# Windowed attention, then a spiking layer: the row-maximum matmuls cut into 64 by 64 tiles and moved ahead of the values, loops written out, and another order of one engine's transfers

## The chip, the cores and the metric

The kernel runs on one core of one Trainium2 chip. The metric is the device time of one execution in microseconds (us). Three runs of the kernel before gave 540.75, 542.55 and 543.64 us; the median is 542.55.

## The reference

The input `x` is (8, 32, 32, 256). Two layers follow each other, each added to its input, each behind a group norm (32 groups of 8 channels, over a whole sample).

```
qkv = part @ qkv_w.T + qkv_b            # part: 8 x 8 windows, 128 windows of 64 tokens, 256 channels
attn = einsum('wihd,wjhd->whij', q * SCALE, k) + bias_table[REL_IDX] + MASK     # 16 heads of 16
out  = softmax(attn) @ v                # per window and head
x = x + out
h = einsum('tbld,hd->tblh', x_normed, W) + b    # t is the sample, 8 steps
# v = v + (h - v) / 2;  spike = v >= 1;  v = 0 where it spiked;  x = x + spike
```

The spikes are thresholds, so the first layer is computed with 16-bit values split into a high and a low part.

## The kernel before

**Tiling.** Channels lie on the 128 partitions in two halves (`HALVES`). A *row* is one row of windows: 4 windows of 64 tokens, 256 tokens; there are 4 rows in a sample and 32 in all. A row is worked on as two *pairs* of windows, so the main loop has 64 pairs, `n`; `k` counts the 8 pairs of a sample, `p` is `k % 2`. In `run`, sample 0 and samples 6 and 7 are written out and samples 1 to 5 are a loop of the engines (`eng.Fori`). Behind the pairs comes the spiking layer, in `lif_units`, looped in the same way by `over_y`.

**Engines.** Each engine has its own program in a fixed, hand-written order; semaphores tie them. In pair `n` TensorE (PE) runs: the projections of the next row (q and k where `p` is 0, v where it is 1), `scores(n)`, the values of the pair before (`weigh_values(n - 1)`, L1005), the maxima's scores of the next pair (`max_scores(n + 1)`, L949 and L955), and the turning of an attention result (L1015). The softmax needs each query's maximum before the exponential: `max_scores` computes scores from the high parts alone with queries on the partitions, VectorE (DVE) reduces them (`maxima`, L756), PE turns the result (L989, in the middle of `scores`), ScalarE (ACT) copies it to `max_rows` (L570), and 8 matmuls with `pick_max` (L982) subtract it from the scores. ACT then takes two exponentials for each of the two banks (L579, L580), and GpSimd (POOL) makes the low part (L426).

**Transfers.** `scores` multiplies stacks of 96 partitions: 32 rows each of the parts high, low, high of q against high, high, low of k. SyncE (SP) builds them: it writes q and k of the next row to memory (`q_spill`, `k_spill`), spreads q's high part into `q_hi` for `max_scores` (4 issues), and reads the stacks back (`q_stack`, `k_stack`, 3 issues each). `scores` of a row's first pair waits on `stacked`; `max_scores` of it on `q_spread`. All these go through one queue, and x of the sample after next (L332) follows on it.

**Norms.** Once in a sample the statistics of the next one run beside pairs k = 1 to 3; POOL takes the roots at k = 2 (`norm_roots`), ahead of `xn_lo` (L388), for which the q projection waits.

## Time and profile before

| | |
|---|---|
| median of 3 runs | 542.55 us |
| the profiled execution, its time | 539.22 us |
| the profiled execution, its span | 537.5 us |
| PE busy | 455.3 us, 85% of the span |
| DVE, ACT, POOL busy | 429.5, 394.3, 272.7 us |
| PE's granted clock, mean | 0.978 |

Times in the rows are microseconds from the start of the span unless they are marked ns. A row of a timeline has start, duration, engine, line, operation and tiles, and in brackets the idle time of that engine before it and what ended it. Matmul durations hold the time through the array; the pace of back-to-back matmuls is the distance of their starts. PEld is the weight load of PE. "SPq" rows are the issues of transfers by SyncE.

### The profile page before, as it was taken

To read this page: it belongs to the slowest core of one execution; us is meant where nothing else is said; L and a number is where in the kernel's file an instruction comes from. 1 tells how busy PE (TensorE), PEld (TensorE's weight loads), DVE (VectorE), ACT (ScalarE), POOL (GpSimd) and SP (SyncE) were. 2 spreads that over 40 slices of the span, in tenths; PEclk is the share of its full clock that TensorE was granted. 3 is DMA by queue.
4 is the path that set the end of the run, shared out by engine and by line. 5 is a ranking of instruction groups with operands and counts; after the bars stand their busy time and mean duration, and the time that the engine had idled before them with its cause. 6 is when DMAs were issued, how large, how long until landed. Compare 5 with 4: busy or idle time off the path is not lost.

```text
span 537.5 us, 17535 instructions
## 1 busy us (share of the span) xinstructions
PE 455.3 (85%) x6504; PEld 417.5 (78%) x6504; DVE 429.5 (80%) x864; ACT 394.3 (73%) x885; POOL 272.7 (51%) x370
## 2 busy tenths in 40 slices
PE   0274799888999899989998998999899977789996
PEld 0164688888889788978887887898788866678885
DVE  8856568877888788878887898789777877488887
ACT  1375568877888788878887888788888856665551
POOL 6132466557555756666656566665655555540000
PEclk9988779999999999999999999999999989999999
DMA  6257066676777667767776778675666655023333
GB/s 194 80 153 194 8 177 175 165 201 171 186 180 180 173 180 185 211 149 209 198 198 161 195 195 200 159 190 157 160 160 168 163 142 157 3 84 132 137 137 138
DMA packets 92574, 86.07 MB, mean 160 GB/s; under 512 B 41842, under 2 KB 63604, under 8 KB 92532
## 3 DMA queue, kind: packets, MB, share of 16 engines
q1 hardware_dynamic: 91808, 85.49, 59.5%
q8 instruction: 27, 0.44, 0.4%
q10 hardware_dynamic: 724, 0.01, 0.1%
q14 instruction: 15, 0.12, 0.1%
HBM read 47.72 MB, written 33.55 MB: 151 GB/s over the span
## 4 chain that ended last, share of the span: by engine, by line
PE 37%; issue 16%; POOL 15%; ACT 9%; DVE 9%; DMA 8%; SPq 4%; POOLq 1%; ACTq 0%; DVEq 0%
POOL p_lo L426 7%; PE pv_ps L1005 4%; DMA k_stack<-k_spill1lo 3%; POOL xn_lo L388 3%; PE score_ps L982 3%; POOL xc L415 3%; PE proj_ps L905 3%; DMA k_spill1lo<-k_lo 3%; PE proj_ps L892 3%; PE pv_ps L892 3%; PE score_ps L892 3%; PE proj_ps L907 3%; PE proj_ps L906 3%; SPq L311 2%; PE max_ps L955 2%
## 5 line engine op out<-in xcount | busy, mean ns | idle before, releaser
L426 POOL TENSOR_TENSOR p_lo<-probs,p_hi 128x512 f16<-128x512 f32 x128 | 146.6, 1166 | 150.8 <-ACT p_hi L580 150.8
L579 ACT ACTIVATE probs<-score_ps 128x512 f32<-128x512 f32 x128 | 77.0, 601 | 18.4 <-PE score_ps L982 17.6
L905 PE MATMUL proj_ps<-xn_hi,w_hi 128*128 128x256 f32 x256 | 77.3, 302 | 14.2 <-POOL xn_lo L388 14.2
L972 PE MATMUL score_ps<-both_parts,bias_k 128*128 128x64 f16 x1024 | 78.2, 193 | 10.7 <-DMA k_stack<-k_spill1lo 6.3
L972 PEld LDWEIGHTS score_ps<-both_parts,bias_k 128*128 128x128 f16 x1024 | 69.7, 98 | 15.8 <-issue 7.8
L756 DVE TENSOR_REDUCE neg_max<-max_ps 128x16 f16<-128x1024 f32 x64 | 78.4, 1224 | 4.2 <-PE max_ps L955 2.1
L974 PE MATMUL score_ps<-q_stack,k_stack 96*128 96x64 f16 x1024 | 77.9, 193 | 0.0
L580 ACT ACTIVATE p_hi<-score_ps 128x512 f16<-128x512 f32 x128 | 77.4, 605 | 0.0
L906 PE MATMUL proj_ps<-xn_lo,w_hi 128*128 128x256 f32 x256 | 74.1, 290 | 0.0
L907 PE MATMUL proj_ps<-xn_hi,w_lo 128*128 128x256 f32 x256 | 73.4, 287 | 0.0
L974 PEld LDWEIGHTS score_ps<-q_stack,k_stack 96*128 96x128 f16 x1024 | 69.1, 98 | 0.0
L739 DVE SCALAR_TENSOR_TENSOR k_lo<-proj_ps,parity_mask,k_hi 128x512 f16<-128x512 f32 x64 | 45.1, 747 | 27.6 <-ACT k_hi L494 27.6
L750 DVE TENSOR_TENSOR v_lo<-proj_ps,v_hi 64x256 f16<-64x256 f32 x128 | 53.9, 421 | 12.9 <-ACT v_hi L502 10.8
L905 PEld LDWEIGHTS proj_ps<-xn_hi,w_hi 128*128 128x128 f32 x256 | 50.5, 197 | 15.9 <-POOL xn_lo L388 9.0
L502 ACT ACTIVATE v_hi<-proj_ps 64x256 f16<-64x256 f32 x128 | 50.3, 393 | 9.2 <-PE proj_ps L917 7.7
L770 DVE TENSOR_TENSOR attn<-pv_ps,recip 64x256 f32<-64x256 f32 x128 | 54.0, 422 | 3.1
L1005 PE MATMUL pv_ps<-v_hi,p_hi 128*128 128x68 f16 x512 | 55.9, 197 | 0.5 <-POOL p_lo L426 0.5
L1005 PE MATMUL pv_ps<-v_hi,p_lo 128*128 128x68 f16 x512 | 56.1, 197 | 0.0
L1005 PE MATMUL pv_ps<-v_lo,p_hi 128*128 128x68 f16 x512 | 56.0, 196 | 0.0
L982 PE MATMUL score_ps<-max_rows,pick_max 128*128 128x128 f16 x512 | 40.6, 224 | 18.1 <-ACT max_rows L570 16.4
L494 ACT ACTIVATE k_hi<-proj_ps,parity_mask 128x512 f16<-128x512 f32 x64 | 40.5, 684 | 20.0 <-PE proj_ps L907 20.0
L949 PE MATMUL max_ps<-bias_q,ident_h 128*128 128x512 f16 x128 | 50.0, 391 | 3.7 <-ACT bias_q L510 3.7
(137 smaller groups left out, 1349.3 us busy)
## 6 DMA issues: line engine op xcount, KB each, us to landing
xc<-in_x_dram SPq DMA_DIRECT2D x32, 256.0 KB, 4.8
k_stack<-k_spill0hi SPq DMA_DIRECT2D x32, 256.0 KB, 4.2
k_stack<-k_spill1hi SPq DMA_DIRECT2D x32, 256.0 KB, 4.0
out_dram<-xc SPq DMA_DIRECT2D x32, 256.0 KB, 2.3
q_hi<-q_flat SPq DMA_DIRECT2D x128, 32.0 KB, 2.0
k_spill0hi<-k_hi SPq DMA_DIRECT2D x16, 256.0 KB, 2.2
k_spill0lo<-k_lo SPq DMA_DIRECT2D x16, 256.0 KB, 2.4
q_stack<-q_spill0hi SPq DMA_DIRECT2D x32, 128.0 KB, 2.7
```

The lines of the kernel that those rows point to most:

```text
L426: pool.tensor_tensor(p_lo[p][:, quads, :, :].rearrange("p g w i -> p (g w i)"), probs[:, quads, :, :].rearrange("p g w i -> p (g w i)"), p ...
L579: act.activation(probs[:, quads, :, :].rearrange("p g w i -> p (g w i)"), score_ps[:, h, :], ACT.Exp)
L580: act.activation(p_hi[p][:, quads, :, :].rearrange("p g w i -> p (g w i)"), score_ps[:, h, :], ACT.Exp)\
L756: dve.tensor_reduce(neg_max[:, 0:16], max_ps[:, :, :].rearrange("p w (n j) -> p (w n) j", j=WS), AX.X, ALU.max, negate=True).then_inc(neg_ ...
L770: last = dve.tensor_tensor(attn[k % 2][rows, :, :, :], heads[rows, :, w, :, 0:D], recip[rows, :, w, :].unsqueeze(3).to_broadcast([WS, HALV ...
L905: pe.matmul(dst, w_hi[:, c, cols], high[:, tok], start=(c == 0 and bias is None), stop=False)
L906: pe.matmul(dst, w_hi[:, c, cols], low[:, tok], start=False, stop=False)
L907: last = pe.matmul(dst, w_lo[:, c, cols], high[:, tok], start=False, stop=(c == HALVES - 1))
L972: pe.matmul(dst, bias_k[:, variant(k, w), h * QUADS + g, :], both_parts[:, 0, :], start=(g == 0 and w == 0), stop=False)
L974: pe.matmul(dst, k_stack[slot][:, g, at, :], q_stack[slot][:, g, at, :], start=False, stop=False)
L982: last = pe.matmul(dst, pick_max[:, 4 * w + 2 * h + mid, :], max_rows[p][:, :].rearrange("p (q i) -> p q i", q=2), start=False, stop=(w == ...
L1005: last = pe.matmul(cols[:, :, g, :], pp[p][:, h * QUADS + g, :, :].rearrange("p w i -> p (w i)"), vv[k // 2][:, p, h * QUADS + g, :, :, :] ...
```

## The change

Four things change together.

1. `max_scores` and the `pick_max` matmuls are cut into tiles of 64 by 64: the contraction runs over one half of the partitions and the output lies on one half. The two halves of the partitions (pairs of quads, `mid`) now write two different banks of `max_ps` and of `score_ps`, where before a bank held a window or a half of the heads. The 2 bias matmuls of 512 columns and 8 of 128 become 8 of 256 and 16 of 128; the 8 `pick_max` matmuls of 128 columns become 16. `bias_q`, `pick_max` and the reading patterns of DVE and ACT are laid out to match.
2. On PE `max_scores(n + 1)` runs right behind the `pick_max` matmuls, ahead of `weigh_values(n - 1)`; on DVE `maxima(n + 1)` runs ahead of `attention_out(n - 1)`. The waits of both tile groups stand before the last ordinary matmul of `scores`.
3. `run` and `over_y` are written out: no engine loops any more.
4. SP's order in `move_q_and_k`: k's high part is spilled between the spreads of two quads each, and the stacks are read in the order q high twice, k high twice, q low, k low, each with a semaphore of its own.

```diff
-            for k in range(BODY):
-                body(k, k // 2, k, 0)
-            with eng.Fori(1, SAMPLES - 2) as s:
-                for k in range(BODY):
-                    body(s * BODY + k, s * WROWS + k // 2, k, s)
-            for s in (SAMPLES - 2, SAMPLES - 1):
+            for s in range(SAMPLES):
                 for k in range(BODY):
                     body(s * BODY + k, s * WROWS + k // 2, k, s)
...
+                landed = slot_total(row, y, 16)
                 sp.wait_ge(q_flat_done, done)
...
+                sp.dma_start(q_spill[slot][0], q_flat[:, 0, :]).then_inc(q_hi_spilled[slot], 16)
+                spread((0, 1))
                 sp.wait_ge(q_lo_done, done)
...
+                sp.dma_start(q_spill[slot][1], q_flat[:, 1, :]).then_inc(q_lo_spilled[slot], 16)
+                sp.wait_ge(k_hi_done, done)
+                spill_k(0, k_hi, k_hi_spilled)
+                spread((2, 3))
+                sp.wait_ge(k_lo_done, done)
+                spill_k(1, k_lo, k_lo_spilled)
+                sp.wait_ge(q_hi_spilled[slot], landed)
+                stack(0, q_stack[slot], q_spill[slot][0])
+                stack(2, q_stack[slot], q_spill[slot][0])
+                sp.wait_ge(k_hi_spilled[slot], landed)
+                stack(0, k_stack[slot], k_spill[slot][0])
+                stack(1, k_stack[slot], k_spill[slot][0])
+                sp.wait_ge(q_lo_spilled[slot], landed)
+                stack(1, q_stack[slot], q_spill[slot][1])
+                sp.wait_ge(k_lo_spilled[slot], landed)
+                stack(2, k_stack[slot], k_spill[slot][1])
...
-                dve.tensor_reduce(neg_max[:, 0:16], max_ps[:, :, :].rearrange("p w (n j) -> p (w n) j", j=WS), AX.X, ALU.max,
+                dve.tensor_reduce(neg_max[:, :].rearrange("p (m n) -> p m n", m=2)[:, :, 0:8],
+                                  max_ps[:, :, :].rearrange("p m (n j) -> p m n j", j=WS), AX.X, ALU.max,
...
+            def max_scores(k):
+
+                slot = k // 2 % 2
+                halves = [slice(r * WS, (r + 1) * WS) for r in range(2)]
                 for w in range(2):
...
+                    for mid, rows in enumerate(halves):
+                        for q, queries in enumerate(halves):
+                            pe.matmul(max_ps[queries, mid, w * 256:(w + 1) * 256], ident_h[rows, rows],
+                                      bias_q[rows, variant(k, w), q, :, :].rearrange("p h n -> p (h n)"),
+                                      start=(w == 0), stop=False)
+                for w in range(2):
                     wx = 2 * (k % 2) + w
                     for h in range(HALVES):
...
+                        at = (2 * w + h) * 128
+                        for mid, rows in enumerate(halves):
+                            for q, queries in enumerate(halves):
+                                last = pe.matmul(max_ps[queries, mid, at:at + 128], q_hi[slot][rows, h, wx, 2 * mid + q, :],
+                                                 k_hi[slot][rows, h, wx, :, :].rearrange("p e j -> p (e j)"),
+                                                 start=False, stop=(w == 1 and h == 1))
...
+                                if (mid, h, q, w) == (1, 1, 1, 1):
+                                    before_tiles()
+                                pe.matmul(dst, k_stack[slot][:, 2 * mid + q, at, :], q_stack[slot][:, 2 * mid + q, at, :],
+                                          start=False, stop=False)
...
+                        for mid, rows in enumerate(halves):
+                            for e, keys in enumerate(halves):
+                                dst = score_ps[keys, mid, :].rearrange("p (h q w i) -> p h w q i", h=2, q=2, w=2)[:, h, w, :, :]
+                                last = pe.matmul(dst, pick_max[rows, 2 * w + h, keys],
+                                                 max_rows[p][rows, :].rearrange("p (q i) -> p q i", q=2),
+                                                 start=False, stop=(w == 1 and h == 1))
+                            if w == 1 and h == 1:
+                                last.then_inc(score_ps_done, 1)
```

**Order on PE, end of `scores` of a pair.** `score_ps`, `max_ps` and `pv_ps` are the banks of the scores, of the maxima's scores and of the values. Before:

```order
L974 MATMUL score_ps<-q_stack,k_stack 128x64
L982 MATMUL score_ps<-max_rows,pick_max 128x2x64 [waits max_rows_done]
L982 MATMUL score_ps<-max_rows,pick_max 128x2x64 x7
L1005 MATMUL pv_ps<-v_hi,p_hi 128x2x34 [waits attn_done,p_lo_done]
...
L949 MATMUL max_ps<-bias_q,ident_h 128x512 [waits bias_q_done,max_rows_done]
L955 MATMUL max_ps<-k_hi,q_hi 128x128 x4
```

and the same place now:

```order
L997 MATMUL score_ps<-q_stack,k_stack 128x64 [waits bias_q_done,max_rows_done]
L1007 MATMUL score_ps<-max_rows,pick_max 64x2x64 x16
L966 MATMUL max_ps<-bias_q,ident_h 64x256 x8
L975 MATMUL max_ps<-k_hi,q_hi 64x128 x16
L1031 MATMUL pv_ps<-v_hi,p_hi 128x2x34 [waits attn_done,p_lo_done]
```

The two tile groups stand together, the wait for `max_rows` has moved one matmul forward, and the values come behind both.

**Order on DVE, a pair with the norm's variances.** `neg_max` is the reduction of the maxima, `root_guess` the start of POOL's roots, `recip` and `attn` the division of the values. Before:

```order
L739 SCALAR_TENSOR_TENSOR k_lo<-proj_ps,parity_mask,k_hi 128x8x64
L689 TENSOR_SCALAR tiny<-pv_ps 128x2 [waits norm_pe,pv_ps_done]
L692 TENSOR_SCALAR root_guess<-tiny 128x2 [waits norm_dve]
L766 RECIPROCAL recip<-pv_ps 128x32
L770 TENSOR_TENSOR attn<-pv_ps,recip 64x256 [waits recip_done]
L770 TENSOR_TENSOR attn<-pv_ps,recip 64x256
L756 TENSOR_REDUCE neg_max<-max_ps 128x16 [waits max_ps_done]
```

and now:

```order
L750 SCALAR_TENSOR_TENSOR k_lo<-proj_ps,parity_mask,k_hi 128x8x64
L767 TENSOR_REDUCE neg_max<-max_ps 128x2x8 [waits max_ps_done]
L699 TENSOR_SCALAR tiny<-pv_ps 128x2 [waits norm_pe,pv_ps_done]
L702 TENSOR_SCALAR root_guess<-tiny 128x2 [waits norm_dve]
L778 RECIPROCAL recip<-pv_ps 128x32
```

The reduction has moved ahead of everything that needs the values' bank.

**Order on SP, the transfers of one row.** Before:

```order
L308 DMA q_spill0hi<-q_flat 128x512 [waits q_flat_done]
L311 DMA q_hi<-q_flat 32x8x64 x4
L314 DMA q_spill0lo<-q_flat 128x512 [waits q_lo_done]
L317 DMA k_spill0hi<-k_hi 128x1024 [waits k_hi_done]
L317 DMA k_spill0lo<-k_lo 128x1024 [waits k_lo_done]
L303 DMA q_stack<-q_spill0hi 32x4x512 [waits q_spilled0]
L303 DMA q_stack<-q_spill0lo 32x4x512
L303 DMA q_stack<-q_spill0hi 32x4x512
L303 DMA k_stack<-k_spill0hi 32x4x1024 [waits k_spilled0]
L303 DMA k_stack<-k_spill0hi 32x4x1024
L303 DMA k_stack<-k_spill0lo 32x4x1024
```

and now:

```order
L314 DMA q_spill0hi<-q_flat 128x512 [waits q_flat_done]
L304 DMA q_hi<-q_flat 32x8x64 x2
L317 DMA q_spill0lo<-q_flat 128x512 [waits q_lo_done]
L308 DMA k_spill0hi<-k_hi 128x1024 [waits k_hi_done]
L304 DMA q_hi<-q_flat 32x8x64 x2
L308 DMA k_spill0lo<-k_lo 128x1024 [waits k_lo_done]
L298 DMA q_stack<-q_spill0hi 32x4x512 [waits q_hi_spilled0]
L298 DMA q_stack<-q_spill0hi 32x4x512
L298 DMA k_stack<-k_spill0hi 32x4x1024 [waits k_hi_spilled0]
L298 DMA k_stack<-k_spill0hi 32x4x1024
L298 DMA q_stack<-q_spill0lo 32x4x512 [waits q_lo_spilled0]
L298 DMA k_stack<-k_spill0lo 32x4x1024 [waits k_lo_spilled0]
```

The number of issues is the same; k's high part leaves two issues earlier, half of the spread leaves later, and no read of a high part waits for the write of a low one.

## Rows read from the trace of the kernel before

**Rows 1.** The page: busy time, share of the span, instructions.

```profile
PE 455.3 (85%) x6504; PEld 417.5 (78%) x6504; DVE 429.5 (80%) x864; ACT 394.3 (73%) x885; POOL 272.7 (51%) x370
```

**Rows 2.** Waits of the whole execution: us in total, times, longest.

```profile
PEld score_ps L982 <- ACT max_rows L570: 23.0, 40, 5.1
...
PE proj_ps L905 <- POOL xn_lo L388: 14.2, 8, 6.8
...
PE max_ps L989 <- DVE neg_max L756: 7.5, 9, 1.8
...
PE score_ps L972 <- DMA k_stack<-k_spill1lo: 6.3, 7, 2.3
...
PE score_ps L972 <- DMA k_stack<-k_spill0lo: 4.0, 4, 2.2
```

**Rows 3.** Timeline of PE, one row of windows inside the loop.

```profile
249.71 0.20 PE L972 MATMUL score_ps<-both_parts,bias_k 128*128 128x64 f16 x1
...
250.75 0.19 PE L974 MATMUL score_ps<-q_stack,k_stack 96*128 96x64 f16 x1
251.36 0.62 PE L982 MATMUL score_ps<-max_rows,pick_max 128*128 128x128 f16 x8 [0.41 <-ACT max_rows L570]
251.82 0.20 PE L1005 MATMUL pv_ps<-v_hi,p_hi 128*128 128x68 f16 x1
...
252.57 0.38 PE L949 MATMUL max_ps<-bias_q,ident_h 128*128 128x512 f16 x1
...
253.45 0.39 PE L1015 MATMUL proj_ps<-ident,attn 128*128 128x128 f32 x2
...
256.43 0.62 PE L982 MATMUL score_ps<-max_rows,pick_max 128*128 128x128 f16 x8
```

**Rows 4.** Timeline of ACT, the same stretch.

```profile
249.90 1.27 ACT L494 ACTIVATE k_hi<-proj_ps,parity_mask 128x512 f16<-128x512 f32 x2 [0.55 <-PE proj_ps L907]
251.06 0.25 ACT L570 ACTIVATE max_rows<-max_ps 16x128 f16<-16x128 f16 x1
```

**Rows 5.** Timeline of DVE, a pair with the norm's variances.

```profile
228.83 1.22 DVE L756 TENSOR_REDUCE neg_max<-max_ps 128x16 f16<-128x1024 f32 x1
```

**Rows 6.** Timeline of POOL, around the roots of a sample.

```profile
226.47 2.28 POOL L426 TENSOR_TENSOR p_lo<-probs,p_hi 128x512 f16<-128x512 f32 x2 [3.90 <-ACT p_hi L580]
...
233.03 1.26 POOL L388 TENSOR_TENSOR xn_lo<-xn,xn_hi 128x512 fp32r<-128x512 f32 x1
```

**Rows 7.** Timeline of PE: the q projection behind the roots, three samples.

```profile
131.52 0.38 PE L905 MATMUL proj_ps<-xn_hi,w_hi 128*128 128x256 f32 x1 [1.18 <-POOL xn_lo L388]
...
183.39 0.38 PE L905 MATMUL proj_ps<-xn_hi,w_hi 128*128 128x256 f32 x1 [1.18 <-POOL xn_lo L388]
...
234.35 0.38 PE L905 MATMUL proj_ps<-xn_hi,w_hi 128*128 128x256 f32 x1 [1.18 <-POOL xn_lo L388]
```

**Rows 8.** Timeline of SP: one row's transfers, inside the loop.

```profile
249.38 0.34 SPq L308 DMA_DIRECT2D q_spill0hi<-q_flat  x1
249.77 2.57 SPq L311 DMA_DIRECT2D q_hi<-q_flat  x4
...
254.39 0.32 SPq L303 DMA_DIRECT2D q_stack<-q_spill0hi  x1
...
255.88 0.78 SPq L303 DMA_DIRECT2D k_stack<-k_spill0hi  x2
256.71 0.43 SPq L303 DMA_DIRECT2D k_stack<-k_spill0lo  x1
```

**Rows 9.** Timeline of SP: one row's transfers, code written out.

```profile
375.61 0.34 SPq L308 DMA_DIRECT2D q_spill0hi<-q_flat  x1
...
378.90 1.82 SPq L314 DMA_DIRECT2D q_spill0lo<-q_flat  x1
...
384.57 0.44 SPq L303 DMA_DIRECT2D k_stack<-k_spill0lo  x1
```

**Rows 10.** The page, DMA issues: xcount, KB each, us from issue to landing.

```profile
k_stack<-k_spill0lo SPq DMA_DIRECT2D x16, 256.0 KB, 5.1
```

More of the change, by code:

```diff
@@ L251, in over_y @@
         def over_y(eng, body):
-            body(0)
-            with eng.Fori(1, WROWS - 1) as y:
+            for y in range(WROWS):
                 body(y)
-            body(WROWS - 1)
         BODY = 2 * WROWS
@@ L304, in stack, with spread, spill_k @@
                                  src.rearrange("(g r) n -> r g n", g=QUADS)).then_inc(stacked[slot], 16)
+                def spread(quads):
+                    for g in quads:
+                        rows = slice(32 * g, 32 * g + 32)
+                        sp.dma_start(q_hi[slot][rows, :, :, g, :].rearrange("p h w i -> p (h w) i"),
+                                     q_flat[rows, 0, :].rearrange("p (n i) -> p n i", i=WS)).then_inc(q_spread[slot], 16)
+                def spill_k(part, keys, spilled):
+                    sp.dma_start(k_spill[slot][part], keys[slot][:, :, :, :, :].rearrange("p h w e j -> p (h w e j)"))\
+                      .then_inc(spilled[slot], 16)
@@ L634, in _ @@
             dve.wait_ge(mask_step, 6)
-            dve.tensor_copy(pick_max[:, :, :].rearrange("p v (e j) -> p (v e) j", e=2),
-                            ident_h[:, 0:16].unsqueeze(2).to_broadcast([128, 16, WS]))
+            for r in range(2):
+                half = slice(r * WS, (r + 1) * WS)
+                dve.tensor_copy(pick_max[half, :, :].rearrange("p v (e j) -> p (v e) j", e=2),
+                                ident_h[half, r * WS:r * WS + 8].unsqueeze(2).to_broadcast([WS, 8, WS]))
             for buf in (v_hi[1], v_lo[1]):
@@ L776, in _ @@
             bias_variant(1)
-            q_low(1)
+            q_low(0, 1)
             k_low(0, 1)
@@ L806, in pair @@
                     norm_moments(norm, x1_stats, SAMPLES - 1)
+                if not is_last_pair(n):
+                    maxima(n + 1)
                 beside = None
@@ L951, in max_scores @@
                     wx = 2 * (k % 2) + w
                     for h in range(HALVES):
-                        for mid in range(2):
-                            at = (2 * h + mid) * 128
-                            last = pe.matmul(max_ps[:, w, at:at + 128],
-                                             q_hi[slot][:, h, wx, 2 * mid:2 * mid + 2, :].rearrange("p q i -> p (q i)"),
-                                             k_hi[slot][:, h, wx, :, :].rearrange("p e j -> p (e j)"),
-                                             start=False, stop=(h == 1 and mid == 1))
+                        at = (2 * w + h) * 128
@@ L1041, in pair, with await_tile_operands @@
                     pe.wait_ge(bias_lo_done, variant(k, 1) + 1)
-                scores(n, row, k)
+                following = (n + 1, row + 1 if p else row, (k + 1) % BODY)
+                def await_tile_operands():
+                    pe.wait_ge(max_rows_done, n + 1)
+                    if not is_last_pair(n):
+                        await_max_operands(*following)
+                scores(n, row, k, await_tile_operands)
                 norm, _, width, stage = norm_beside(s, k)
```

95 lines of the change are left out of this document (36 added, 59 removed).

## The prediction

> **What bounds the kernel now.** I read the page first: PE is busy 455.3 of 537.5 us [rows 1], more than any other engine, so matmul time counts, if nothing else paces the rows. Then the list of waits, which says what PE waited for [rows 2]: `max_rows` from ACT, `xn_lo` from POOL, `neg_max` from DVE, and the last stack of k's low part. Then the timeline of one row of windows [rows 3]. The reader is to see that PE is nearly gapless: `scores` starts at 249.71, its last matmul at 250.75, then PE idles until ACT's copy ends at 251.31 [rows 4], takes 251.36 to 251.82 for the 8 `pick_max` matmuls (0.46 us), 0.75 for the values, 0.88 for the maxima's scores (252.57 to 253.45), and the next pair's `pick_max` is at 256.43. The first wait is ACT's, not PE's: ACT gets k from PE at 249.90, needs 1.16 us to the start of its copy, and only then copies [rows 4].
>
> Two chains run beside it. **The stacks:** from the spill of q (249.38) to the issue of the last stack (256.71) are 7.33 us [rows 8], plus 5.1 to its landing [rows 10], so 12.4 us; it lands at 261.8. The distance from one row to the next on PE is about 12.15 us, so from 249.71 PE wants the stack at 261.86. That is a tie: whatever PE saves in a row is worth nothing beyond that tie unless the stacks also come sooner. Because q of the row after next is projected before `scores` of the next row has started, two rows share it: two rows take (work from scores to the q spill after next) + (spill to landing), 11.9 + 12.4. **The roots:** once a sample, POOL goes from `p_lo` at 226.47 over the roots to `xn_lo`, ended at 234.29 [rows 6], and PE's projection stands at 234.35 behind it, 1.18 us idle [rows 7]. From one such place to the next are 50.96 us (183.39 to 234.35), of which 7.9 are POOL's fixed stretch; PE time saved in that stretch (k = 2 and 3) is lost there. What counts is PE's time in three rows of four.
>
> **The change part by part.**
>
> *Tiles.* Before, a pair costs 0.46 + 0.88 = 1.34 us for both groups [rows 3]. After, there are 40 tile matmuls: 24 for the maxima's scores with 4096 columns in all, 16 for `pick_max` with 2048. No row shows tiles. Lower bound: all four tiles run abreast, 1536 columns; 1024 columns now take 0.46 us, so 0.69 us, a saving of 0.65. Upper bound: none do, 6144 columns at that pace, 2.76 us, a loss of 1.42. Between stands the pace of matmuls too short to be bound by columns: 249.71 to 250.75 is 33 starts in 1.04 us, 0.0325 each [rows 3]; 40 of them are 1.3 us, a saving of nothing. Weight loads of different tiles should partly overlap, so I take 0.9 us, midway between 0.69 and that: saving 0.44. Each pair also enters and leaves the tiles. If the array has to empty, the next matmul starts when the one before has come through: a short matmul lasts 0.20 where the pace is 0.03, so up to 0.17 each way, at least nothing. I take 0.08 each, 0.16 a pair. Net **0.28 us a pair, 0.56 a row** (bounds: +0.65 and, with only loads serial and a full drain, -0.3).
>
> The Trainium skill ("TensorEngine Tiling (Array Packing)", Key Properties) says that changing the tiling mode drains the engine, and (Restrictions) that column tiling turns fast weight load off. No row of before has a tile. By that rule the drain is the full 0.17 each way and the net is about 0.1 a pair instead of 0.28. The same skill ("TensorE: Matmul & The Clock Gate", Part 3) states that packed matmuls start about 4 ns apart; by that the saving before the drain would be the 0.65 of the lower bound. The sum stands on the rows.
>
> *Order on PE and DVE.* `maxima` (1.22 us) goes ahead of the division. PE waits 7.5 us in all for `neg_max` [rows 2]. In samples 1 to 5 these waits stand in k = 3 (DVE starts the reduction at 228.83, behind the roots' guess [rows 5]), inside POOL's stretch, and give nothing there. In the last sample nothing covers them: I take 1.5 us. The division comes 1.2 us later; `weigh_values` of the next pair needs it over 2 us later than it ends now, so no cost; it would cost the difference if PE came that close. The values' matmuls come later by the length of the tile group, about 0.6 us, under the same cover.
>
> *SyncE.* The stacks' issues no longer wait for low parts: those gaps are 0.4 us ahead of 254.39 and 0.2 ahead of 255.88 [rows 8], and 0.2 to 0.4 comes back for k's low part. k's high part leaves about 1.3 us earlier (two spreads of 0.64), while the queue is still light, so some 0.7 us of transfer is gone from the full stretch. Bounds 0.2 and 1.1 us sooner; I take **0.6**. Against it: the second half of the spread now lands later, and `q_spread` is awaited before `pick_max` of the odd pair (256.43), not before 257.6. Issue is by 253.4 at best, landing about 2 to 3 us on, 255.4 to 256.4; a tie again, which I put at nothing.
>
> *Loops.* Written-out code issues transfers more slowly: from q's spill to the last stack are 8.96 us against 7.33 in the loop [rows 9, 8], with one issue of 1.82 us where others take 0.6. I read that as the program being fetched through queues that are full. The loop's first pass shows the price in time: 131.52 to 183.39 is 51.87 us, where the next sample takes 50.96 [rows 7], so **0.9 us a sample**, for samples 2 to 5; samples 0, 1, 6 and 7 pay it already. Turning back costs nothing that can be seen.
>
> *Sum.* A sample from 2 to 5: three rows' 2 x 0.28 = 0.56 each would be 1.7 if PE alone set the pace. By the stack chain, which passes twice between two root stretches, it is 2 x 0.6 sooner + 0.56 from PE - 0.9 for written-out code = 0.9. I take 0.9: 3.6 us for four. Sample 1: its rows wait for stacks (most of the 10.3 us in [rows 2] lies in written-out code and the first pass), so 1.8. Samples 0, 6 and 7: 1.1 each, 3.3. The last sample's `neg_max`: 1.5. Together 10.2 us off 539.2, so 529.0 for an execution such as the profiled one. The median of the runs is 3.3 above the profiled one, so the prediction is **532 us**.
>
> **The rivals.**
>
> *A, only the transfers' order helps.* Tile matmuls go at the short-matmul pace of 0.0325 us and the drains are whole: 1.3 + 0.34 against 1.34, a loss of 0.3 a pair, half hidden in the waits ahead of `pick_max` (0.41 and 0.2). Then PE is 0.3 a row slower, the stacks come 0.6 sooner and 0.9 a sample goes to written-out code: -2 to +3, about 542, no change. The weight loads speak for it: PEld is busy 78% [rows 1]. Chance 0.20.
>
> *B, the tiles run fully abreast.* Saving 0.65 less 0.05 for the switches, 0.6 a pair; the rows then run at the stacks' pace or at ACT's (0.55 idle in [rows 4] is ACT's slack for a pair). 3 x 1.2 a sample as the most, cut by the stack tie to some 2.5, eight samples 20 us, and 1.5: 521 us. The skill's 4 ns speaks for it. Chance 0.20.
>
> *C, slower: the tiles do not overlap.* Tiles of one bank or one half wait for each other, so that two thirds of the columns go singly: 2.0 + 0.2 against 1.34, 0.9 a pair. Past about 0.3 a pair PE passes the tie with the stacks and each further 0.1 costs 0.1 x 6 x 8 = 5 us; 0.9 would give 543 + 29 = 570. A weaker form is the spread: if it lands 1 us past the end of the odd pair's scores, 32 rows pay up to 1 us, less what the stacks' tie gave: 555. Chance together 0.14. It decides from 1.7 us for both groups of a pair.
>
> *D, written-out code costs more than one first pass showed*, since PE, too, fetches about twice as many instructions: 2 us a sample would eat the whole gain: 541. Chance 0.08.
>
> **How the numbers follow.** The forecast (520 to 539) has 0.38, A 0.20, B 0.20, C 0.14, D 0.08. A measurement of this kernel tells about 0.5%, 2.7 us, from no change. Faster by more than that (below 539.8): the forecast 0.37, B 0.20, a part of A and D 0.06, together 0.63. The same: 0.18. Slower: C's 0.14 and part of A and D, 0.19. The range leaves out the lower third of B and most of C: 518 to 549. The forecast's own range is 525 to 538.
>
> **What would show it.** In the profile after, the distance from the first `pick_max` tile to the first values' matmul should be 0.9 to 1.1 us for both groups (0.7 is B, 1.3 and more A, 2 C). PE should wait for stacks in fewer rows than before, but still in some; the spill-to-last-stack distance should be about 8 us in all samples, with one long issue in most rows. The sample distance should be about 50.1 us. The wait for `xn_lo` should grow to 2 to 2.5 us a sample, and that for `neg_max` go. I am wrong if PE waits at the last matmul of `scores` for the spread, or if the row distance falls under 11.6 us.

## The result, and the profile after

The changed kernel takes 554.88 us (median of 4 runs, 550.02 to 556.45), against 542.96 for the kernel before in the same comparison (4 runs, 540.75 to 543.64). The ratio is 1.0203, 95% interval 1.0158 to 1.0249: **2% slower**, where 2% faster was forecast. A second measurement of six executions gave 551.73 and 1.0156 (1.0107 to 1.0205), so what is sure is a loss of 1 to 2.5%. The profiled execution took 553.81 us, its span 551.8.

The page of the changed kernel: the span, busy time by engine, then the two queues that bring instructions (packets, MB, share of the 16 DMA engines), then two rows of the issues with KB and us to landing.

```profile
span 551.8 us, 19279 instructions
...
PE 441.6 (80%) x7912; PEld 409.0 (74%) x7912; DVE 423.2 (77%) x865; ACT 392.0 (71%) x885; POOL 272.9 (49%) x370
...
q8 instruction: 63, 1.03, 0.9%
q14 instruction: 24, 0.20, 0.1%
...
k_stack<-k_spill0lo SPq DMA_DIRECT2D x16, 256.0 KB, 5.4
...
k_stack<-k_spill1lo SPq DMA_DIRECT2D x16, 256.0 KB, 5.7
```

PE is 13.7 us less busy than before [rows 1] and the span is 14.3 us longer, so the added time is waiting. The page of the kernel before had 27 packets on q8 and 15 on q14, now there are 63 and 24. (The experiments below show whose they are: q8 goes from 27 to 51 when PE's program alone is written out, and stays at 27 when SyncE's is.) The landing of the last stack of either slot, 5.1 [rows 10] and 5.0 us before, now takes 5.4 and 5.7.

The waits of PE (us in total, times, longest):

```profile
PE score_ps L993 <- DMA k_stack<-k_spill1lo: 22.5, 14, 3.7
PE proj_ps L917 <- POOL xn_lo L396: 22.5, 8, 6.8
PE score_ps L997 <- ACT max_rows L578: 18.2, 29, 5.0
...
PE score_ps L993 <- DMA k_stack<-k_spill0lo: 6.1, 6, 1.4
PE score_ps L997 <- DMA q_hi<-q_flat: 4.3, 5, 1.3
```

Beside [rows 2]: the waits for the stacks of k have gone from 10.3 to 28.6 us, those for `xn_lo` from 14.2 to 22.5, and there is a new one, 4.3 us, for the late half of the spread of q.

The timeline of PE where a pair goes from `scores` through the tiles to the values:

```profile
245.22 0.19 PE L993 MATMUL score_ps<-both_parts,bias_k 128*128 128x64 f16 x1
245.82 0.20 PE L997 MATMUL score_ps<-q_stack,k_stack 96*128 96x64 f16 x1 [0.41 <-ACT max_rows L578]
245.96 0.42 PE L1007 MATMUL score_ps<-max_rows,pick_max 64*64 64x128 f16 x16
246.20 0.39 PE L966 MATMUL max_ps<-bias_q,ident_h 64*64 64x256 f16 x8
246.42 0.39 PE L975 MATMUL max_ps<-k_hi,q_hi 64*64 64x128 f16 x16
246.75 0.20 PE L1031 MATMUL pv_ps<-v_hi,p_hi 128*128 128x68 f16 x1
```

The 40 tile matmuls take 0.79 us (245.96 to 246.75, the way out of the tiles included) and the entry 0.14, where the two groups took 1.34 [rows 3]. So the tiles do run side by side: at the pace of [rows 3], an estimate, their 6144 columns would have taken 2.76 us one after another and 0.92 three at a time. The distance is 0.78 to 0.80 us in 55 of 63 pairs of this trace. The tiles are not what is slow in this row; what stands around them is.

### The profile page after: what moved, and what is told of

Same layout as the page of the kernel before. It is cut to its first block, busy times and chain, and to the rows that moved or that the text cites. A ratio compares the mean times of both kernels' runs of the same rounds, so it can differ in the third digit from the quotient of the medians.

```text
span 551.8 us, 19279 instructions
## 1 busy us (share of the span) xinstructions
PE 441.6 (80%) x7912; PEld 409.0 (74%) x7912; DVE 423.2 (77%) x865; ACT 392.0 (71%) x885; POOL 272.9 (49%) x370
## 4 chain that ended last, share of the span: by engine, by line
PE 28%; ACT 17%; SPq 17%; DMA 16%; POOL 9%; issue 7%; DVE 5%; ACTq 1%; POOLq 0%; DVEq 0%
DMA k_stack<-k_spill1lo 12%; SPq L304 7%; SPq L298 5%; POOL p_lo L434 3%; PE score_ps L904 3%; SPq L308 3%; ACT p_hi L588 3%; PE proj_ps L917 3%; PE proj_ps L904 3%; PE pv_ps L904 3%; ACT v_hi L510 2%; PE proj_ps L919 2%; ACT attn_cm L551 2%; PE proj_ps L918 2%; ACT xn L471 2%
## 5 line engine op out<-in xcount | busy, mean ns | idle before, releaser
L997 PE MATMUL score_ps<-q_stack,k_stack 96*128 96x64 f16 x1024 | 85.4, 195 | 23.8 <-ACT max_rows L578 18.2
L993 PE MATMUL score_ps<-both_parts,bias_k 128*128 128x64 f16 x1024 | 78.7, 195 | 31.0 <-DMA k_stack<-k_spill1lo 22.5
L917 PE MATMUL proj_ps<-xn_hi,w_hi 128*128 128x256 f32 x256 | 79.2, 309 | 22.5 <-POOL xn_lo L396 22.5
L997 PEld LDWEIGHTS score_ps<-q_stack,k_stack 96*128 96x128 f16 x1024 | 72.3, 99 | 29.1 <-ACT max_rows L578 26.0
L918 PE MATMUL proj_ps<-xn_lo,w_hi 128*128 128x256 f32 x256 | 76.0, 297 | 0.0
L919 PE MATMUL proj_ps<-xn_hi,w_lo 128*128 128x256 f32 x256 | 75.9, 297 | 0.0
L917 PEld LDWEIGHTS proj_ps<-xn_hi,w_hi 128*128 128x128 f32 x256 | 52.7, 206 | 24.3 <-POOL xn_lo L396 17.3
L761 DVE TENSOR_TENSOR v_lo<-proj_ps,v_hi 64x256 f16<-64x256 f32 x128 | 54.2, 424 | 16.5 <-ACT v_hi L510 14.8
L1031 PE MATMUL pv_ps<-v_hi,p_hi 128*128 128x68 f16 x512 | 58.1, 200 | 0.6 <-POOL p_lo L434 0.6
L1031 PE MATMUL pv_ps<-v_lo,p_hi 128*128 128x68 f16 x512 | 57.9, 198 | 0.0
L1031 PEld LDWEIGHTS pv_ps<-v_hi,p_hi 128*128 128x128 f16 x512 | 50.9, 103 | 5.5 <-POOL p_lo L434 1.0
L918 PEld LDWEIGHTS proj_ps<-xn_lo,w_hi 128*128 128x128 f32 x256 | 52.7, 206 | 0.0
```

Source lines behind the costliest of these rows:

```text
L761: last = dve.tensor_tensor(v_block(v_lo[slot], w, e), v_part(w, e), v_block(v_hi[slot], w, e), ALU.subtract)
L917: pe.matmul(dst, w_hi[:, c, cols], high[:, tok], start=(c == 0 and bias is None), stop=False)
L918: pe.matmul(dst, w_hi[:, c, cols], low[:, tok], start=False, stop=False)
L919: last = pe.matmul(dst, w_lo[:, c, cols], high[:, tok], start=False, stop=(c == HALVES - 1))
L993: pe.matmul(dst, bias_k[:, variant(k, w), h * QUADS + 2 * mid + q, :], both_parts[:, 0, :], start=(h == 0 and q == 0 and w == 0), stop=False)
L997: pe.matmul(dst, k_stack[slot][:, 2 * mid + q, at, :], q_stack[slot][:, 2 * mid + q, at, :], start=False, stop=False)
```

## The experiments

All ratios are to the kernel before, measured beside each kernel on the same chip, with 95% intervals. "Written out" is the change's third part, "transfer order" its fourth, "order" its second (PE and DVE).

**Each part alone.** Written out alone (`run` as below, and the loop of the spiking layer in `over_y` in the same way):

```diff
-            for k in range(BODY):
-                body(k, k // 2, k, 0)
-            with eng.Fori(1, SAMPLES - 2) as s:
...
-            for s in (SAMPLES - 2, SAMPLES - 1):
+            for s in range(SAMPLES):
```

> The kernel before with its engine loops written out, and nothing else. Theory 1 (written-out code: instruction packets share the full transfer queues, issues on SyncE stall and stacks land late): slower by 1.5 to 3.5%, about 551 to 562 us, sample distance in samples 1 to 5 about 52 to 53.5 us instead of 50.96. Theory 2 (the new order of SyncE's transfers costs): within 0.7%, up to 0.9 us a sample, about 543 to 547. Theory 3 (the tiles themselves, or the clock they bring, cost): within 0.5%.

Measured: 550.76 us, ratio 1.0149 (1.0087 to 1.0212), the lower edge of what theory 1 said and above what theories 2 and 3 allowed, with 52 packets on q8.

Transfer order alone, with `move_q_and_k` as in the change and the rest of before:

```diff
+                sp.dma_start(q_spill[slot][0], q_flat[:, 0, :]).then_inc(q_hi_spilled[slot], 16)
+                spread((0, 1))
...
+                spill_k(0, k_hi, k_hi_spilled)
+                spread((2, 3))
```

> The kernel before with the new order of SyncE's transfers alone, loops kept, no tiles. Theory 1: same to faster, -1 to 0%. Theory 2: slower by 1 to 3%, with PE waiting for the spread of q or for the stack of k's low part in most rows. Theory 3: within 0.5%.

Measured: 539.76 us, ratio 0.9953 (0.9919 to 0.9986). In the loop the distance from q's spill to the last stack's issue went from 7.3 to 7.15 us, not by the 0.6 that the prediction took. Theory 2, that this order costs, is out.

The tiles and the order with the loops kept:

```diff
-                            last = pe.matmul(dst, pick_max[:, 4 * w + 2 * h + mid, :],
...
+                        for mid, rows in enumerate(halves):
+                            for e, keys in enumerate(halves):
...
+                                last = pe.matmul(dst, pick_max[rows, 2 * w + h, keys],
```

> The kernel before with tiles and their place ahead of the values alone, loops and transfer order kept. Theory 1 and 2: faster by 0.5 to 2%, because the tile groups take about 0.8 us a pair against 1.34 but the stacks set the pace of most rows; PE waits longer for the stacks than before. Theory 3: slower by 1 to 2%.

Measured: 583.89 us, ratio 1.0793 (1.0730 to 1.0856). The same with the new transfer order:

> The changed kernel with the engine loops kept. Theory 1: the full gain of the other parts, -2 to -4%, about 522 to 532 us, issue of one row's transfers 7.0 us long inside the loop. Theory 2: about 0 to +2%. Theory 3: +1% or more.

Measured: 575.82 us, ratio 1.0579 (1.0494 to 1.0663). Theories 1 and 2 missed by far; theory 3, that the tiles cost, had the sign both times, but said 1 to 2% for the first. The queue of PE's instructions, q8, said where to look: 68 packets in each, more than the 63 of the changed kernel, although the loops were kept.

**Is it the tiles, or the length of the loop?** The kernel before, cut into as many matmuls as the tiles need, without any tile:

```diff
-                    pe.matmul(max_ps[:, w, :], ident_h[:, :], bias_q[:, variant(k, w), :, :].rearrange("p m n -> p (m n)"),
+                    for m4 in range(4):
+                        pe.matmul(max_ps[:, w, m4 * 128:(m4 + 1) * 128], ident_h[:, :], bias_q[:, variant(k, w), m4, :],
...
+                            for e in range(2):
...
+                            for q in range(2):
```

> The kernel before, loops kept, with the matmuls of the maxima's scores and of the maxima's subtraction cut by columns into as many as the tiles need (2 of 512, 8 and 8 of 128 columns become 8 of 128, 16 and 16 of 64), all still over 128 partitions: the tiles' number of instructions without tiles. At 0.0325 us for a short matmul the groups take 40 x 0.0325 = 1.3 us as before. Theory (TensorE's loop body has outgrown what stays in reach, and is fetched anew in each pass): instruction packets on PE's queue rise from 27 to about 68, PE stands about 3 us at each turn of the loop, 570 to 585 us, ratio 1.05 to 1.08. Rival (the tiles themselves made the looped kernel slow): packets may rise a little, 541 to 548 us, ratio 0.997 to 1.01.

Measured: 582.49 us, ratio 1.0714 (1.0666 to 1.0762). The page's queues and two kinds of waits of this kernel, and one turn of the loop on PE's timeline:

```profile
q8 instruction: 68, 1.11, 0.9%
```

```profile
PE proj_ps L905 <- issue: 12.2, 4, 3.6
...
PEld score_ps L974 <- issue: 22.2, 12, 2.8
```

```profile
163.62 0.38 PE L905 MATMUL proj_ps<-xn_hi,w_hi 128*128 128x256 f32 x1 [2.89 <-issue]
```

Without a tile in it the kernel shows the whole loss. "Issue" means that PE waited for nothing that the profile shows; with 68 packets I read it as waiting for instructions. Four times, at the turn from one sample to the next, PE stands 2.8 to 3.6 us, 12.2 us in all; the kernel before has no such wait. The late weight loads of L974 come to 22.2 us in 12 places, where L972 of the kernel before has 7.8 in 10. The changed kernel has as many matmuls as this one, written out, and is 1.6 to 2% slower, not 7%: so it is neither the tiles nor the number of matmuls, but a longer body in a loop.

A smaller step past the same edge, with tiles only for `pick_max` and both orders, 10 more matmuls for a pair instead of 22:

```diff
                 for w in range(2):
                     for mid in range(2):
+                        pe.matmul(max_ps[:, mid, w * 256:(w + 1) * 256], ident_h[:, :],
```

> Loops kept, SyncE's new order, the new order of PE and DVE; tiles of 64 by 64 only where the maxima are subtracted (8 matmuls become 16), the maxima's scores in matmuls over 128 partitions (2 of 512 columns become 4 of 256). That is 10 added matmuls for a pair, not 22. Theory (a loop body of TensorE that is 20% longer no longer stays, one that is 10% longer may): if it stays, 27 to 30 packets and 535 to 540 us, ratio 0.985 to 0.995; if it doesn't, 60 packets and 560 to 575. Rival (any tiles cost more than they save, by the switching): 27 to 30 packets and 545 to 550.

Measured: 579.58 us, ratio 1.0659 (1.0599 to 1.0718), 65 packets, and four waits of PE for "issue" of 23.4 us in all at the turns of the loop. This body does not stay either; the expectation for that case, 560 to 575 us and 60 packets, was still too low.

**Whose written-out code costs?**

```diff
+            if eng is nc.tensor:
+                for s in range(SAMPLES):
+                    for k in range(BODY):
+                        body(s * BODY + k, s * WROWS + k // 2, k, s)
+                return
```

The other kernel has `nc.sync` in place of `nc.tensor`. Both leave the loop of the spiking layer (`over_y`) as it is.

> The kernel before, with TensorE's code alone written out; all other engines keep their loops. Theory 1 (the cost of written-out code is the fetching of PE's instructions: its stalls and its packets on the queues that the stacks use): most of the 7.8 us of the kernel with all loops written out, 548 to 551, ratio 1.009 to 1.015, 15 to 20 more instruction packets. Rival (the cost is SyncE's, whose long issues of 1.2 to 1.9 us come from its own code being fetched): 542 to 544, ratio 1.000.

> The kernel before, with SyncE's code alone written out; all other engines keep their loops. Theory 1 (fetching of PE's instructions costs): 542 to 544, ratio 1.000, spill to last stack 7.2 to 7.6 us as in the loop. Rival (SyncE's own issues become long): spill to last stack 8.4 us in samples 1 to 5 and 547 to 550, ratio 1.008 to 1.013.

Measured: PE alone 547.96 us, ratio 1.0105 (1.0062 to 1.0147), 51 packets; SyncE alone 544.54, ratio 1.0034 (1.0005 to 1.0064), 27 packets. In samples 2 to 5 the distance from q's spill to the last stack (16 rows of SyncE's timeline) is 8.5 us on average with PE written out and 7.4 with SyncE written out (7.4 before). The queue of PE's instructions and the waits for the stacks, with PE alone written out:

```profile
q8 instruction: 51, 0.84, 0.7%
```

```profile
PE score_ps L977 <- DMA k_stack<-k_spill1lo: 14.7, 14, 2.1
...
PE score_ps L977 <- DMA k_stack<-k_spill0lo: 5.3, 7, 1.2
```

That is 20.0 us of waits for the stacks where the kernel before has 10.3 [rows 2], and 24 packets more where 15 to 20 were expected. SyncE's timeline, with PE written out and SyncE's own code still in its loop:

```profile
243.19 0.32 SPq L308 DMA_DIRECT2D q_stack<-q_spill1hi  x1
243.55 1.58 SPq L308 DMA_DIRECT2D q_stack<-q_spill1lo  x1
245.17 0.43 SPq L308 DMA_DIRECT2D q_stack<-q_spill1hi  x1
246.25 0.78 SPq L308 DMA_DIRECT2D k_stack<-k_spill1hi  x2
247.06 0.43 SPq L308 DMA_DIRECT2D k_stack<-k_spill1lo  x1
```

One issue of 1.58 us where the next of its kind takes 0.43: the long issues that the prediction saw in [rows 9] come with the fetching of another engine's program. The code outside `run` has a part, too: from the last matmul of `scores` to the end of the span are 74.5 us before, 74.2 with PE's `run` written out, and 76.2 with everything written out, `over_y` included (one profiled execution each).

**The steps from written-out code to the change.**

> The kernel before with the loops written out and SyncE's new order of transfers; no tiles, PE and DVE in the old order. Theory 1 (the parts add up: written-out code costs 1.5%, the transfer order gives 0.5% back): 548 us, ratio 1.010. Rival (in written-out code the stacks are what PE waits for, so that sooner stacks are worth more there than in the loop): 543 to 545, ratio 1.000 to 1.004. Second rival (with more instruction packets on the same engines the reads land at the same time whatever their order): 550 to 551, ratio 1.015.

Measured: 551.21 us, ratio 1.0184 (1.0122 to 1.0246). The spill-to-stack distance fell from 8.7 to 8.0 us, and the time did not follow it: the theory's ratio of 1.010 and the first rival's 1.000 to 1.004 both lie outside the interval, and the second rival's 551 is what came. Its reason did not: PE waits 15.7 us for the stacks instead of 19.0. Against written-out code alone (1.0149) the intervals overlap, so all that is shown is that the new order has no gain here that can be seen.

```diff
+                if not is_last_pair(n):
+                    max_scores(n + 1, row + 1 if p else row, (k + 1) % BODY)
                 if not is_first(n, 1):
                     weigh_values(n - 1, row if p else row - 1, (k - 1) % 4, beside)
-                if not is_last_pair(n):
-                    max_scores(n + 1, row + 1 if p else row, (k + 1) % BODY)
```

> The whole change without the tiles: loops written out, SyncE's new order, and on PE and DVE the maxima ahead of the values and of the division, in the old matmuls of 128 by 128. Against the changed kernel this is the price of the tiles alone. Theory 1 (the order of PE and DVE is worth what I predicted, 1.5 us, and the tiles' 7 added matmuls and loads for each one removed cost more in fetched instructions and stack waits than the 0.4 us a pair that they save): 545 to 548, ratio 1.004 to 1.010, that is 7 to 10 us under the changed kernel. Rival (the order itself costs, since the spread is awaited earlier and the values' bank comes later): 552 to 556, ratio 1.017 to 1.024, tiles worth about nothing.

Measured: 549.66 us, ratio 1.0108 (1.0064 to 1.0152), just above the theory's range, and 5 us under the changed kernel instead of the 7 to 10 expected. The two orders with loops kept:

> The kernel before, loops kept, no tiles, with SyncE's new order and the new order of PE and DVE. Theory (the parts add up: 0.5% from the transfers' order and the 1.5 us of the waits for neg_max, and little more, since in samples 1 to 5 those waits lie in POOL's stretch): 536 to 539 us, ratio 0.988 to 0.993. Rival (the earlier wait for the spread of q costs what the order gives): 539 to 542, ratio 0.995 to 1.000.

Measured: 541.87 us, ratio 0.9954 (0.9926 to 0.9981), the same as the transfer order alone. The theory's 0.988 to 0.993 missed and the rival's 0.995 to 1.000 came, though not for the rival's reason: PE never waits for the spread of q in this profile. The order of PE and DVE shows no gain here; the wait for `neg_max` falls from 7.5 to 1.9 us, that for `xn_lo` grows from 14.2 to 18.2 and that for `max_rows` from 16.4 to 19.4.

**What the tiles cost in written-out code.** Four kernels side by side on one chip: the change again, the change without tiles, with filler matmuls at the roots (matmuls whose result nobody reads), and with the old transfer order. The kernel without tiles also keeps the old layout of the banks and the old places of the waits: in the changed kernel PE waits for `max_rows` and for the spread of q ahead of the last ordinary matmul of `scores`. What is called the price of the tiles below is the price of all three.

> The changed kernel itself once more, beside the others of this call. Both theories: ratio 1.016 to 1.025, mean granted clock 0.945 to 0.960, span times clock 522 to 528 us.

> The changed kernel without its tiles once more (loops written out, both new orders, matmuls over 128 partitions), beside the changed kernel on one chip. Theory (the tiles save some 6 us of work at the full clock and lose 10 to 12 us to the clock that falls behind PE's longer gaps): ratio 1.008 to 1.014, 3 to 6 us under the changed kernel, clock 0.97, span times clock 530 to 532. Rival (the earlier distance of 5 us was chance): within 2 us of the changed kernel.

```diff
+                if filler:
+                    for i in range(8):
+                        pe.matmul(banks[6], ident_h[:, :], bias_k[:, i % 4, 0:4, :].rearrange("p g n -> p (g n)"),
+                                  start=True, stop=True)
                 pe.wait_ge(xn_lo_done, r + 1)
```

`filler` holds where `k == 4` and `1 <= s <= 6`.

> The changed kernel with 8 matmuls of 512 columns that nobody reads ahead of the wait for xn_lo at the roots of samples 1 to 6 alone, where PE waits 1.5 to 2.6 us each time, so that they delay little. Theory (the falls of the clock behind these waits cost time; two of the five falls in the profiled run stood there): clock 0.958 to 0.968, 2 to 4 us under the changed kernel, ratio 1.012 to 1.017. Rival (the lower clock falls into time that PE would wait out): clock higher, time within 1 us of the changed kernel.

> Tiles, both engines' order and written-out loops with SyncE's order of before. Theory (with the stacks as what PE waits for, an order that ends 0.1 to 0.3 us sooner is worth 0.3% or nothing beside the waits for the late half of the spread, 4.3 us): within 3 us of the changed kernel, ratio 1.018 to 1.030. Rival (the late spread is what the tiles lose by): 3 to 5 us under the changed kernel, ratio 1.010 to 1.015, no wait for q_hi at the last matmul of the scores.

The table has medians, and means of the clock and the two last columns over the executions of each kernel (without one of 1129 us of the kernel before and one of 1482 us of the kernel without tiles). The fourth column is span times (1 - mean granted clock), the fifth span times the clock: what the span would be if all work had gone at the full clock and every lost tick had counted.

| kernel | median us, ratio (interval) | clock | lost to the clock | rest |
|---|---|---|---|---|
| before | 542.37 | 0.976 | 12.7 | 528.0 |
| the change | 551.73, 1.0156 (1.0107 to 1.0205) | 0.950 | 27.3 | 522.2 |
| without tiles | 547.60, 1.0102 (1.0051 to 1.0153) | 0.973 | 15.0 | 530.8 |
| filler at the roots | 549.86, 1.0138 (1.0084 to 1.0193) | 0.958 | 23.1 | 524.6 |
| old transfer order | 558.84, 1.0317 (1.0268 to 1.0367) | 0.944 | 31.2 | 525.5 |

The tiles cost 4 us here (the means are 3.8 apart, 95% interval 1.0 to 6.5) and 5 in the first pair of measurements. By the table they take 8.6 us out of the rest and put 12.3 into the clock's column. Between 90 and 430 us the profile of the changed kernel has five falls of the clock, which take 8 us (span times 1 - clock, read in steps of 2 us); the kernel without tiles has none there in this profile and one in its other. What such a stretch looks like, on PE's timeline of the changed kernel:

```profile
239.50 0.39 PE L917 MATMUL proj_ps<-xn_hi,w_hi 128*128 128x256 f32 x1 [2.56 <-POOL xn_lo L396]
...
240.68 0.28 PE L917 MATMUL proj_ps<-xn_hi,w_hi 128*128 128x256 f32 x1
240.80 0.29 PE L918 MATMUL proj_ps<-xn_lo,w_hi 128*128 128x256 f32 x1
240.92 0.39 PE L919 MATMUL proj_ps<-xn_hi,w_lo 128*128 128x256 f32 x1
241.11 0.41 PE L914 MATMUL proj_ps<-ones_r,b_rows 128*128 128x256 f32 x1
241.32 0.41 PE L917 MATMUL proj_ps<-xn_hi,w_hi 128*128 128x256 f32 x1
```

and its windows (length, busy time of PE, PEld, DVE, ACT, POOL with counts, then granted clock, DMA share, GB/s):

```profile
239.40:241.00 1.60, 1.50 (x12) 1.50 (x13) 0.48 (x2) 0.01 (x1) 1.60 (x3) 0.98 0.06 15
241.00:244.00 3.00, 3.00 (x16) 3.00 (x15) 0.88 (x2) 0.84 (x2) 1.38 (x2) 0.50 0.17 49
```

PE waits 2.56 us, starts at the full clock, and 1.4 us later the clock falls to 1.2 GHz: matmuls follow each other at 0.21 us instead of 0.12. PE has no gap in these 3 us, so what the clock costs there, about half of them, is PE's own time. The same behind a wait of 1.96 us for a stack (335.63) meets the tiles:

```profile
336.97 0.64 PE L1007 MATMUL score_ps<-max_rows,pick_max 64*64 64x128 f16 x16
337.39 0.64 PE L966 MATMUL max_ps<-bias_q,ident_h 64*64 64x256 f16 x8
337.82 0.64 PE L975 MATMUL max_ps<-k_hi,q_hi 64*64 64x128 f16 x16
```

Here the groups start 0.42 and 0.43 us apart, where they were 0.24 and 0.22 apart above. The kernel before had no such stretch between 90 and 430 us. A long wait does not always bring a fall: at the roots PE waits 2.3 to 2.6 us five times after 100 us, and the clock fell behind two of these (130.65 and 239.50). "TensorE: Matmul & The Clock Gate" of the Trainium skill (HAM oscillation) describes kernels in which waits for transfers make the clock fall again and again. These rows agree in that the clock falls behind waits, one for a transfer and one for POOL; they differ in that the work behind the wait starts at the full clock and falls 1.4 us later.

Filling 8 matmuls into the waits at the roots took 4.2 us out of the clock's column and 1.9 us off the median. In its profile no fall between 90 and 430 us stands behind a root, and four stand elsewhere. That points the way the theory says, but the intervals overlap, so the fillers alone do not prove it. A kernel with 4 fillers ahead of each stack too:

> The changed kernel with matmuls whose result nobody reads, put where PE waits: 8 of 512 columns ahead of the wait for xn_lo at the roots of samples 1 to 6, and 4 of 512 columns ahead of each row's wait for the stacks from sample 1 on. Theory (part of the tiles' price is the clock, which falls to its lower level behind PE's longer gaps): mean granted clock 0.965 to 0.975 where the changed kernel had 0.956, 549 to 553 us, ratio 1.012 to 1.018. Rival (the lower clock lies in stretches where PE would wait anyway, and costs nothing): the clock rises and the time stays at 554 or grows by the fillers' own 0.9 us where a stack has landed already, up to 560.

Measured: 551.03 us, ratio 1.0171 (1.0125 to 1.0216), clock 0.970; 16.7 us lost to the clock, rest 531.1 (means without its slowest execution, 554.54 us). The clock came back and the time did not: the rest is 9 us more than the changed kernel's. That these are the fillers' own time where a stack had landed already is a reading; no run separates it.

The old transfer order removes the wait for `q_hi` and is 7 us slower than the change, outside both the theory (within 3 us) and the rival (3 to 5 us faster). So with tiles the new order as a whole is worth 1.6%. It does not clear the late spread: the old order also brings the stacks later, and PE waits 32.8 us for them, as much as for the stacks and the spread together in the changed kernel (28.6 and 4.3).

**What stays open about the tiles.** The clock has a rival that no run parts from it. The waits for the stacks in the kernel without tiles:

```profile
PE score_ps L981 <- DMA k_stack<-k_spill1lo: 9.4, 7, 4.1
PE score_ps L981 <- DMA k_stack<-k_spill0lo: 6.9, 6, 1.6
```

That is 16.3 us against 28.6 with tiles (26.9 in the second profile), and none for `q_hi` against 4.3 and 5.6. The distance from q's spill to the last stack in samples 2 to 5 is 7.9 and 8.1 us in the two profiles without tiles and 8.3 and 8.5 in the two with them, with 52 and 63 packets. So the tiles' instructions may lengthen SyncE's issues as PE's written-out program does, and the moved waits may cost; a kernel with as many matmuls, written out and without tiles, was not run, nor one with tiles and the waits in their old places.

## Why the prediction was wrong

**The failed step is the sum for a sample: "2 x 0.6 sooner + 0.56 from PE - 0.9 for written-out code = 0.9".** All three terms failed, and the two gains by more than the cost. Outside the 3.6 us for written-out code the prediction counted 13.8 us of gains (10.2 + 3.6). Measured, both orders together take 2 to 3 us off written-out code (1.0149 to 1.0108 or 1.0102, intervals that overlap), and the tiles add 4 to 5 us. So 15 to 18 of the 20 to 22 us between forecast and measurement lie in the gains that did not come, and about 4 in the price of written-out code.

The stack chain that the prediction used shows where: the time from q's spill to the landing of the last stack was to fall by 0.6 from 12.4 us, with the price of written-out code beside it; it rose to about 14.0 (8.5 to the issue and 5.4 or 5.7 more). By the prediction's own formula, an estimate, twice 1.6 us a sample make 54.2 us from root to root; the five distances between 77 and 347 us are 53.5 to 55.3. The measured time also lies outside all three ranges that the prediction gives (520 to 539, 525 to 538, 518 to 549), and of its rivals none had this pair of causes: D's 541 was too low, and C's 555 comes near by luck, since the tiles do overlap and the spread costs PE 4.3 us in five rows, not up to 1 us in 32.

**"0.9 us a sample, for samples 2 to 5".** The prediction priced written-out code by one comparison inside the kernel before [rows 7] and got 3.6 us. Measured, it is 7.8 us, ratio 1.0149. For samples 2 to 5 the sample distance, at the end of the roots, went from 50.96 to between 52.1 and 52.8 us, and the distance that ends in sample 1 (78.7 to 131.5 before) grew by 2.6 us. The prediction had this as rival D, with 0.08. The mechanism was right as far as it went: fetching the program slows the transfers of the stacks. Whose program it is the sum did not say; it is PE's, as rival D had it, 27 packets before and 52 written out, and PE alone carries most of the loss (1.0105 of 1.0149). Nor did the sum have a term for the spiking layer's loop. One first pass was a weak source for the price: the last distance between roots in the kernel before, whose second half is written out, is 50.89 us and shows none at all.

**The tiles: gain under-estimated, price missing.** The prediction took 0.9 us for both groups and 0.16 for the switches, a saving of 0.28 a pair. Measured, 0.79 and an entry of 0.14 where matmuls otherwise follow at 0.03, a saving of about 0.44; the exit lies in the 0.79. That was rival B's mechanism, in part. "TensorEngine Tiling (Array Packing)" of the Trainium skill (Key Properties) says that changing the mode drains the engine; the entry of 0.14 us is in keeping with that, though no run tells a drain from a late weight load, and it is no great price. What lacked in the sum was what 1408 more matmuls, and as many loads, do away from PE's own line: 11 more packets (52 to 63), and longer gaps, behind some of which the clock falls. The prediction said that "whatever PE saves in a row is worth nothing beyond that tie"; it stopped there. Saved time turned into gaps, and the kernel with tiles is 4 to 5 us slower. That the clock's column grows by more than the rest shrinks is measured. That the clock is the cause is argued, from rows in which PE has no gap; how much of that column lies on the path, and how much of the price is the later stacks or the moved waits, stays open.

**"SyncE: I take 0.6 sooner".** 0.15 in the loop, 0.7 in written-out code (8.7 to 8.0). The time followed it unevenly: 0.5% alone, nothing that can be seen in written-out code without tiles, 1.6% with tiles. "A tie again, which I put at nothing" for the spread was wrong in place: PE waits at the last matmul of `scores` for it, 4.3 us in 5 rows, the very sign named for being wrong.

**"Spill to last stack about 8 us in all samples"** came true, 8.5 us on average, with a long issue in most rows. **The stack chain and its landing** were taken as 5.1 us throughout; they are 5.4 to 5.7.

**"The last sample's `neg_max`: 1.5"** went, as forecast (7.5 to 1.9 us of waits, of the whole execution), and showed in no total: both orders looped give the same ratio as the transfer order alone.

**"Turning back costs nothing"** is right for the loop of before alone. With 10 or 22 more matmuls a pair the looped kernel is about 7% slower, so writing the loops out was not a free part of the change: with these tiles it takes 1.058 to 1.016 or 1.020.

**The sample distance** should have been 50.1 us; it is 52.1 to 55.3. By parts: loops and both orders without tiles 1.0 to 1.1%, and the tiles, taken as the difference to the changed kernel, 0.5 to 1%.

**A version that beats both** is the kernel before with the new transfer order alone, loops kept: 539.76 us, ratio 0.9953 (0.9919 to 0.9986).

## What to carry to other kernels

Count the instructions of a hot engine before adding to them: a split that is free on the array can push a loop body past the length that stays, or load the queues that carry the data. Time saved on an engine that already waits turns into gaps, and a gap on TensorE can cost more than its own length where the clock falls behind it: in the rows above 3 us of matmuls ran at half the clock behind a wait of 2.56 us. Price written-out code by a kernel that is written out, not by a first pass.

## What the runs showed of the hardware

- **A loop body of TensorE stays up to a length.** Writing out 4 more samples of PE's program costs 24 packets (27 to 51), so a sample is 6 packets of 16 KB (0.44 MB in 27), about 98 KB; in the loop of before it is fetched once. With 22 more matmuls and as many loads a pair (352 instructions a sample, which written out are 11 packets in 8 samples, 1.4 a sample) it is about 7.4 packets, and with 10 more (160 instructions) about 6.6. Both are fetched anew in each pass: 68 and 65 packets. The edge lies between 6 and 6.6, an estimate from these counts. They do not explain all: 65 is more than the 56 or so that eight samples of 6.6 would make.
- "Runtime: NRT & Kernel Launch" of the Trainium skill (Instruction fetch mechanics) gives PE an instruction memory of 128 KiB, filled in blocks of 16 KiB, calls the crossing of a block mostly hidden, and says that a taken branch whose target is not in the window breaks the prefetch and stalls the engine, one reason why kernels prefer full unrolling. The packets of 16 KB agree, and so do the standstills of 2.8 us and more at the turns of the longer loops. By the 128 KiB alone bodies of 6.6 and 7.4 packets (108 and 121 KB) would have stayed, and they did not. The cost was not hidden, and the advice fails here for the shorter body: unrolling it cost 1.5%.
- **One engine's code lengthens another's transfer issues**: 0.43 to 1.58 us on SyncE while its own code was looped and PE's was written out; with SyncE's alone written out the chain of issues kept its 7.4 us.
- **Tiles of 64 by 64 run side by side, at nearly the pace of four**: 4096 columns in 16 and 8 matmuls and 2048 in 16 more took 0.79 us, where four abreast would be 0.69 and three 0.92 at the pace of [rows 3]; one of the groups of 16 took 0.24.
